# Attention operands in two 12-bit parts and float32r, two heads in each half of the partitions

## The reference

```python
Q = (x @ Wq.T).reshape(H, b, s, 8); K, V likewise              # L0
atten = softmax(einsum('hbqd,hbkd->hbqk', Q, K)); out = atten @ V
q = rope(qkv[0]); k = rope(qkv[1])                             # L3
attn = softmax(einsum('bhqd,bhkd->bhqk', q, k) / sqrt(8)); out = attn @ v
```

## Time and profile before

| | |
|---|---|
| median of 3 runs | 1930.44 us (1928.12 to 1937.29) |
| span of the profiled execution | 1933.0 us (no other time of that execution is given) |
| PE busy | 1543.6 us, 80% |
| DVE busy | 1245.7 us, 64% |
| ACT busy | 1023.7 us, 53% |
| POOL busy | 787.7 us, 41% |
| DMA | 85.19 MB, mean 44 GB/s |

### The profile page before, as it was taken

One profiled execution on the slowest core, in us unless ns is written; L12 is line 12 of the kernel. 1 busy time (PEld: TensorE's weight loads), 2 busy tenths in 40 slices (PEclk: granted clock), 3 DMA queues, 4 the chain that ended last, 5 costly groups with the idle time before them and its releaser, 6 DMA issues. The chain is left out here.

```text
span 1933.0 us, 25902 instructions
## 1 busy us (share of the span) xinstructions
PE 1543.6 (80%) x8437; PEld 813.4 (42%) x8437; DVE 1245.7 (64%) x2976; ACT 1023.7 (53%) x2001; POOL 787.7 (41%) x1504
## 2 busy tenths in 40 slices
PE   2799999996258884747743982599999999799997
PEld 1133333321137773636632661133333333477776
DVE  3688888885565653046558625788888888344453
ACT  2277777775523432246624321177777777554543
POOL 3555555522524555157342675324444431111120
PEclk9699999998585665866656996599999999999999
DMA  4222222210011001100024232211111111100000
GB/s 118 72 64 65 65 66 65 66 38 1 0 56 56 1 13 29 29 10 4 1 56 127 36 39 52 82 50 56 64 59 67 62 61 38 46 6 6 12 12 12
DMA packets 86555, 85.19 MB, mean 44 GB/s; under 512 B 35990, under 2 KB 69632, under 8 KB 86292
## 3 DMA queue, kind: packets, MB, share of 16 engines
q1 hardware_dynamic: 75498, 75.15, 12.1%
q0 software_dynamic: 7680, 6.06, 2.0%
q10 hardware_dynamic: 3242, 2.32, 0.4%
HBM read 59.76 MB, written 25.17 MB: 44 GB/s over the span
## 5 line engine op out<-in xcount | busy, mean ns | idle before, releaser
L937 DVE TENSOR_REDUCE arena<-psum 128x2 f32<-128x1024 f32 x512 | 601.6, 1216 | 104.9 <-PE psum L730 100.2
L842 ACT ACTIVATE arena<-psum 128x512 f32<-128x512 f32 x1024 | 553.5, 595 | 138.1 <-PE psum L743 129.3
L730 PE MATMUL psum<-arena 72*128 72x512 bf16 x1024 | 287.8, 397 | 47.7 <-DMA arena<-L_k_parts 19.0
L743 PE MATMUL psum<-arena 99*128 99x512 bf16 x1024 | 311.9, 386 | 11.5 <-issue 7.2
L753 PE MATMUL psum<-arena 128*32 128x512 f32 x2048 | 274.5, 608 | 3.1 <-ACT arena L842 1.9
L743 PEld LDWEIGHTS psum<-arena 99*128 99x128 bf16 x1024 | 74.7, 98 | 288.4 <-ACT arena L842 223.2
L2452 POOL TENSOR_SCALAR arena<-arena 128x4 f32<-128x4 f32 x112 | 29.4, 263 | 391.5 <-DVE arena L2446 386.9
L730 PEld LDWEIGHTS psum<-arena 72*128 72x128 bf16 x1024 | 95.2, 99 | 191.1 <-DVE arena L937 29.0
L2481 ACT ACTIVATE arena<-arena 128x128 f32<-128x128 f32 x208 | 85.3, 481 | 137.8 <-POOL arena L2458 121.0
L636 POOL TENSOR_TENSOR arena<-arena 128x16 bf16<-128x16 f32 x64 | 14.1, 221 | 293.1 <-DVE arena L937 220.7
L2443 DVE BATCH_NORM_STATS2 arena<-arena 128x6 f32<-128x128 f32 x448 | 96.4, 277 | 57.3 <-PEq L101 21.2
(11 more groups left out here) (437 smaller groups left out, 2475.6 us busy)
## 6 DMA issues: line engine op xcount, KB each, us to landing
arena<-L_q_parts SPq DMA_DIRECT2D x192, 96.0 KB
arena<-L_k_parts SPq DMA_DIRECT2D x180, 96.0 KB
L_q_parts<-arena SPq DMA_DIRECT2D x16, 384.0 KB, 3.3
L_k_parts<-arena SPq DMA_DIRECT2D x16, 384.0 KB, 3.2
arena<-in_L_ffn_w SPq DMA_DIRECT2D x1, 2048.0 KB, 10.8
ec_result<-arena SPq DMA_DIRECT2D x1, 2048.0 KB, 9.8
arena<-in_L_ffn_fc2s SPq DMA_DIRECT2D x1, 2048.0 KB, 17.1
ec_normed<-arena SPq DMA_DIRECT2D x2, 1024.0 KB, 7.5
```

The lines of the kernel that those rows point to most:

```text
L730: last = nc.tensor.matmul(bank[:, 512 * h:512 * h + 512], columns(q9[0:QK_ROWS], i, m // 2, 128 * (2 * (m % 2) + h), 128), columns(k9[0:QK ...
L743: nc.tensor.matmul(acts.bank(name), columns(k9[0:ROWS], i, g, 128 * k, 128), columns(q9[0:ROWS], i, g, 0, 512), start=True, stop=True).the ...
L842: nc.scalar.activation(prob[:, k % 2, g, :], acts.bank(name), ACT.Exp, scale=scale).then_inc(act_taken, 1)
L937: nc.vector.tensor_reduce(neg_max[:, i % 2, 2 * m:2 * m + 2], maxes.bank(("max", i, m)).rearrange("p (h t) -> p h t", h=2), axis=AX.X, op= ...
```

## The change

Two parts instead of three, each a float32r word (an f32 whose mantissa is cut to 12 bits): `PARTS` is 2, so a product has 4 x 8 = 32 rows, a row of ones for the maximum products (33) and two more for the maximum (35 in all). Two heads lie on partitions 0 to 34, two on 64 to 98; neighbouring products on PE use the two halves in turn. Stores are one DMA per part, and keys are stored with their first part twice (`K_SLOTS`), so a load is four DMAs of 32 rows of 4 KB: two for queries, two for keys. The source of each is two blocks (for queries one block twice) of 16 rows, where before it was three of 8. In L3 a store is written as 8 groups of 16 rows instead of 128 rows. Memsets of the operand rows move to the set-up stage. In L3 three rows of ones per half are laid down by two DMAs (`k_ones`) for which PE waits before its first maximum tile. DVE's and PE's order within a step changes a little, and some buffers of other stages move to the new tensor `pairs`.

```diff
+        @block.vector
+        def _(dve):
+            nc.vector.memset(c.q9.rearrange("p s t -> p (s t)").bitcast(I32), 0)
+            nc.vector.memset(c.k9.rearrange("p s t -> p (s t)").bitcast(I32), ONE)
...
-PARTS = 3
-QK_ROWS = PARTS * PARTS * HD
-MAX_ROW = 96
+PARTS = 2
+HALVES = 2
+PRODUCTS = PARTS * PARTS * HD
+MAX_ROW = PRODUCTS + 1
 ROWS = MAX_ROW + PARTS
+LANES = 64
...
-    q_parts = nc.dram_tensor(f"{tag}_q_parts", (B, PARTS, TPB, HD, 2048), BF16).ap()
-    k_parts = nc.dram_tensor(f"{tag}_k_parts", (B, PARTS, TPB, HD, 2048), BF16).ap()
+    K_SLOTS = PARTS + 1
+    q_parts = nc.dram_tensor(f"{tag}_q_parts", (B, TPB, HALVES, PARTS, HD, 1024), F32).ap()
+    k_parts = nc.dram_tensor(f"{tag}_k_parts", (B, TPB, HALVES, K_SLOTS, HD, 1024), F32).ap()
...
+    def columns(rows, height, i, g, first, n):
+        h, e = divmod(g, 2)
+        return rows[LANES * h:LANES * h + height, i % RING, 512 * e + first:512 * e + first + n]
+    def query_rows(i, h):
+        rows = q_parts[i // TPB, i % TPB, h].rearrange("a d t -> (a d) t")
+        return rows.unsqueeze(0).to_broadcast([PARTS, PARTS * HD, 1024])
+    def key_rows(i, h):
+        first = k_parts[i // TPB, i % TPB, h, 0]
+        return bass.AP(first.tensor, first.offset, [[HD * 1024, PARTS], [1024, PARTS * HD], [1, 1024]])
+    def put_max_rows(eng, i):
+        for h in range(HALVES):
+            at = LANES * h + MAX_ROW
+            eng.dma_start(q_words[at:at + PARTS, i % RING, :], max_row[16 * h:16 * h + 16, i % 2, :]).then_inc(max_in[i % RING], 16)
...
-        ch.next(eng.tensor_copy(a[:, 0, :], f))
-        ch.next(eng.tensor_tensor(f, f, a[:, 0, :], ALU.subtract))
-        ch.next(eng.tensor_copy(a[:, 1, :], f))
-        eng.tensor_tensor(a[:, 2, :], f, a[:, 1, :], ALU.subtract).then_inc(part_done[n], 1)
+        eng.tensor_copy(a[:, 0, :].bitcast(F32R), f).then_inc(part_done[n], 1)
+        eng.wait_ge(part_done[n], PARTS * b + 1)
+        eng.tensor_tensor(a[:, 1, :].bitcast(F32R), f, a[:, 0, :], ALU.subtract).then_inc(part_done[n], 1)
...
+                for slot in range((PARTS, K_SLOTS)[n]):
+                    a = slot % PARTS
+                    if by_tokens:
+                        out = dst[:, :, slot].rearrange("t h d (j l) -> (d j) (t h) l", j=HEADS)
+                    else:
+                        out = dst[:, :, slot].rearrange("t h d (e l) -> (t h) (d e) l", e=2)
+                    sp.wait_ge(part_done[n], PARTS * b + a + 1)
+                    sp.dma_start(out, src).then_inc(stored[slot_of(b, n)], 16)
...
-                for p in range(PARTS):
-                    src = q_parts[b, p, s].unsqueeze(0).to_broadcast([PARTS, HD, 2048])
-                    sp.dma_start(q_to[24 * p:24 * p + 24, :], src).then_inc(qk_in[i % RING], 16)
+                for h in range(HALVES):
+                    at = slice(LANES * h, LANES * h + PRODUCTS)
+                    sp.dma_start(q_to[at, :], query_rows(i, h)).then_inc(qk_in[i % RING], 16)
                     if keys:
-                        sp.dma_start(k_to[24 * p:24 * p + 24, :], k_parts[b, :, s]).then_inc(qk_in[i % RING], 16)
+                        sp.dma_start(k_to[at, :], key_rows(i, h)).then_inc(qk_in[i % RING], 16)
...
             store(1, 1)
-            sp.wait_ge(k_pads, 2)
+            if rope:
+                for h in range(HALVES):
+                    at = LANES * h + PRODUCTS
+                    sp.dma_start(k_words[at:at + 1 + PARTS, :, :].rearrange("p s t -> p (s t)"), c.ones[0:32 * (1 + PARTS), :]).then_inc(k_ones, 16)
             load(2)
...
+            if rope:
+                pe.wait_ge(k_ones, 16 * HALVES)
             for i in range(2):
                 operands_set(i)
...
                     if k == 0:
-                        pe.wait_ge(max_in[i % RING], 16 * (i // RING + 1))
+                        pe.wait_ge(max_in[i % RING], 16 * HALVES * (i // RING + 1))
+                        if ahead:
+                            operands_set(i + 2)
                     score_tile(i, k, 0)
-                    score_tile(i, k, 1)
+                    score_tile(i, k, 2)
```

More of the change, by code:

```diff
@@ L6 @@
 BF16 = mybir.dt.bfloat16
+F32R = mybir.dt.float32r
 I32 = mybir.dt.int32
@@ L427, in for_scalar @@
             for k in range(4):
-                for g in range(4):
+                for g in BY_HALVES:
                     yield "score", i, k, g
@@ L645, in _ @@
             of_x.factors(pool, 0)
-            nc.gpsimd.memset(v32[:, :, :, :, HD:32], 1.0).then_inc(k_pads, 1)
-            pool.wait_ge(k_pads, 1)
-            nc.gpsimd.memset(k_words[64:96, :, :].rearrange("p s t -> p (s t)").bitcast(I32), 0).then_inc(k_pads, 1)
-            pool.wait_ge(k_pads, 2)
+            pool.wait_ge(of_x.factors_done, 1)
+            if by_tokens:
+                for h in range(HALVES):
+                    nc.gpsimd.memset(k_raw[pads_of(h), :, :], 1.0).then_inc(k_pads, 1)
+                    pool.wait_ge(k_pads, h + 1)
+            nc.gpsimd.memset(v32[:, :, :, :, HD:32], 1.0).then_inc(v_ones, 1)
+            pool.wait_ge(v_ones, 1)
             if rope:
@@ L727, in max_tile @@
                 pe.wait_ge(max_taken, maxes.room(("max", i, m)))
-                bank = maxes.bank(("max", i, m))
-                for h in range(2):
-                    last = nc.tensor.matmul(bank[:, 512 * h:512 * h + 512], columns(q9[0:QK_ROWS], i, m // 2, 128 * (2 * (m % 2) + h), 128),
-                                            columns(k9[0:QK_ROWS], i, m // 2, 0, 512), start=True, stop=True)
+                g, t = divmod(m, 4)
+                for h in range(HALVES):
+                    last = nc.tensor.matmul(maxes.bank(("max", i, m))[:, 512 * h:512 * h + 512],
+                                            columns(q9, MAX_ROW, i, g + 2 * h, 128 * t, 128),
+                                            columns(k9, MAX_ROW, i, g + 2 * h, 0, 512), start=True, stop=True)
                 last.then_inc(max_made, 1)
@@ L924, in exchange @@
                 if b >= 1:
-                    dve.wait_ge(part_done[n], b)
-                nc.vector.stream_shuffle(other[:, n, :], full[:, n, :], list(range(16, 32)) + list(range(16))).then_inc(exchanged[n], 1)
+                    dve.wait_ge(part_done[n], 2 * b)
+                nc.vector.stream_shuffle(other[:, n, :], full[:, n, :], [i ^ HD for i in range(32)]).then_inc(exchanged[n], 1)
             def operand(b, n):
@@ L979, in _ @@
             order_weights()
-            nc.vector.memset(q_words[64:96, :, :].rearrange("p s t -> p (s t)").bitcast(I32), 0).then_inc(q_pads, 1)
+            if by_tokens:
+                for h in range(HALVES):
+                    nc.vector.memset(q_raw[pads_of(h), :, :], 0.0).then_inc(q_pads, 1)
             if rope:
@@ L2772, in shape_constants @@
     row = np.arange(128)
-    width = row // 4 % HD
+    width = row // 2 % HD
     sign = np.where(width < half, -1.0, 1.0).astype(np.float32)
```

142 lines of the change are left out of this document (69 added, 73 removed).

## The result

The changed kernel takes 2338.99 us (median of 4 runs, 2331.31 to 2353.41), before takes 1931.35: ratio 1.2119, 95% interval 1.2072 to 1.2165. Slower was forecast, but by 36 us; it is 408, and the time lies far outside the range.

What follows compares the result with a forecast made beforehand. PE bounds both attentions now; after the change, loads on two DMA engines were to. L0 +16, L3's start +14, L3's quads +9, last quads -3 make 36 us more: 1966 us, range 1922 to 2005.

Steps and rivals of the forecast that it cites:

- the clock falls: Rival: PE at 1.2 GHz for a third of L3's quads, 25 us more, 1990 us; counted inside the 0.66 case.
- the main case: Both attentions DMA-bound as summed, the low-clock rival inside it; chance 0.66, own range 1945 to 2000 us.
- The forecast's 15.6 us: A quad at 1.2 GHz, from steps of 3.9 us on PE instead of 2.0.
- the sum does not depend on which of these holds: Claim that PE steps of 2.0 or 2.8 us give the same total, since 11.3 per quad is under the DMA's 13.
- Products: PE's float32r products in both attentions: taken to cost as bf16, 0.215 us each, and to run in pairs.
- A step of 2.0 us: PE's step in the attentions with paired products priced as bf16: 4 x 0.215 + 0.86 + 0.25.
- Loads: Deciding term: a quad's four load DMAs run on two engines at 51 GB/s, 10.3 us instead of 7.8.
- the 52.4 that were worked out: Time per L0 batch in us, bound by two DMA engines: 50.0 busy plus 2.4 when the queue runs dry.
- L3's 54.3: Time per L3 batch in us, following the DMA queue, against 53.27 today: +1.0 per batch.
- L3's start: PE waits for rows of ones queued behind two quads' loads and two stores, until 1238.5 instead of 1224.41: +14 us.
- At nothing: Terms priced at zero: set-up memsets, regrouping of 96 rows, shorter splits beside quads, and buffers moved in other stages.

Runs made afterwards that it cites:

- e1: The kernel before with maximum products over 33 of 72 rows and score products over 35 of 99; 2622.5 us.
- e7: The changed kernel with score products over all 64 rows of their half, the added rows zeros in queries and ones in keys; 2073.0 us.
- v7: v2 with DVE's copy of the finished values back between the two reductions, as in the changed kernel; 1946.1 us.
- e10: The changed kernel with only the loads spread over 16 engines and L3's rows of ones written first; 2288.5 us.
- v4: v2 with score products back at 35 rows and maximum products at 33; 2057.3 us, and 2014.4 to 2130.3 us when the same kernel was timed again.
- v2: v1 with each load cut in two DMAs of 16 rows, spread over 16 engines, and L3's rows of ones written first; 1880.7 us, ratio 0.9722.
- v1: The changed kernel with score and maximum products over 64 rows, old maxima cleared, and DVE's copy ahead of both reductions; 2018.9 us, ratio 1.0437.
- v3: v2 with the rows of ones back behind the loads of L3's first two quads and two stores; 1896.6 us, ratio 0.9799.
- v5: The changed kernel with one edit: DVE copies the finished values at a quad's start before both reductions; 2206.4 us.
- e5: The changed kernel plus one overwritten product over 97 rows ahead of the two short ones of each maximum tile; 2772.6 us.
- e8: The kernel before with only its maximum products shortened, from 72 to 33 rows, scores staying at 99; 1978.7 us.
- e2: The changed kernel with score products over rows 0 to 98 and maximum products over rows 0 to 96, so none pair; 2102.6 us.

## Why the prediction was wrong

**The step that failed** is the clock. It stood among the rivals as "the clock falls", inside the main case, for "a third of L3's quads", 25 us, and for none in L0, without a reason given for L0. It was low in most of both attentions. The step at the low clock was about right (3.9 us forecast, 4.07 measured). The extent was not: nearly all of L0 and, by the granted clock of 0.61, about four fifths of L3, instead of 10 quads. Nor was the price of a quad. The forecast's 15.6 us are four steps and nothing else; a quad took 18.9 us on average, of which four steps of 4.07 make 16.3, and projections, turned maxima and waits the rest. With the forecast's own 2.5 us on all of 60 quads it would have said some 2115 us. Of the 223 us that remain the price per quad makes most: 3.3 us more on 62 quads are 205.

Two thoughts led there. The forecast looked for what might lower the clock only in PE's pauses. And it took it that two slow DMA engines make PE's speed irrelevant ("the sum does not depend on which of these holds"), which is true only while PE is faster than they are. e1 shows that short rows do it without any pause, and e7 that filled rows mostly repair it. The changed kernel's L0, where all eight rises of the clock end with the 1.1 us wait, and v7 against e10 show that this pause costs the clock with short products and not with full rows. v4's L0 shows short products at either level for tens of microseconds, without a wait.

That the time came out slower, as forecast, is luck: the slower pace was to come from the loads, which don't set it here.

**Products.** That float32r products cost their columns and pair up was right. "A step of 2.0 us" was wrong even at the full clock: it is 2.67 in v2, from the loop of ACT and PE over three banks. The longer weight loads (183 to 188 ns against 98 at the full clock) were not counted.

**Loads.** Two engines and 51 GB/s were right to the digit. That they bind was wrong for the changed kernel, where PE needs 18.9 us per quad and a load 10, though e10 shows that they cost some us even there. It is right once the clock is back: v1's batches of L0 (52.6 to 54.6 us) come near the 52.4 that were worked out, and spread loads bring them to 47.1 in v3. L3's 54.3 was too low: v1's take 58.5 to 60.0. Its clock also drops in them (0.91 to 0.94 per batch), for which the forecast had 0.5 us.

**L3's start.** From the first load's issue to the first maximum product 30.3 us were forecast (1208.2 to 1238.5), 33.1 came (1424.08 to 1457.21); before it was 12.5. v3 prices the order of the ones alone at 15.9 us, with fast loads. That first load's issue was to be 3.7 us earlier; counted from L0's last quad it is 7.2 later (766.9 us against 759.7). In v1 and v2, whose clock is full at L0's end, it is 760.4 and 760.8, in e10, where it is low, 768.2, so this goes with the clock as well.

**Left out.** The changed order on DVE, with the copy between two reductions, was not in the sum. It is worth 65 us at the full clock (v7 against v2) and 133 in the changed kernel (against v5).

**At nothing.** Regrouping took 1035 ns, now as a cast, as it did before; the term was rightly at nothing. The splits and memsets were not examined alone.

The experiments leave open what in the array decides the clock, beyond that more rows per product bring it up, whether rows count that are zero in both operands, and which small difference decides between the two levels in v4's attentions.

## What to carry to other kernels

When a change makes products shorter in rows or makes PE wait, first price the low clock over the whole stage, with everything that PE does in it: it doubles every product and can last. Products that fill the rows, if need be with zeros in one operand, cost no time here (47.1 us a batch in L0 at the full clock, in v2 as in v4) and kept the clock through pauses of 1.1 us. Then look for the limit behind the one removed (here the loads' two engines, a late copy on DVE, ACT's banks), since a pause that it makes can be paid twice, by itself and by the clock.

## What the runs showed of the hardware

- TensorE stayed at 1.2 GHz for 712 us while it was busy 99.98% of them, with bf16 products over 33 and 35 rows (e1). With the same number over 72 and 99 rows the kernel before has 2.4 GHz from 84 us on.
- Rows that are zero in one operand and one in the other count as rows: 2339 us became 2073 (e7).
- With short products both levels of the clock last. In v4's L0 the granted clock is 0.50 from 78 to 121 us and 1.00 from 122 to 440, with PE busy all the time. The kernel took 2014 to 2057 us, where the others that were timed repeat within 1%.
- A wait of 1.1 us stands at the end of each of the eight stretches of full clock in L0 of the changed kernel; over 64 rows the clock stays through 28 such waits (v7's L0).
- Products over different numbers of rows in alternation start 0.72 us apart at 1.2 GHz instead of 0.43 (e5); among 99-row products, 33-row ones cost 0.2 us per step more than 72-row ones (e8).
- A float32r load of 128 columns of weights takes 183 to 188 ns at the full clock (v2, e2), a bf16 one 98 (before).
